# Splitting the squares of Q and K on GpSimd in place of VectorE, block by block

## The reference

```
dd = einsum('bhnd,md->bhnm', x * data_norm, proj)          # 8 heads of 64, 256 features
diag = 0.5 * sum(x * x, axis=-1) * data_norm ** 2          # per node and head
stab = max(dd) over the features (queries) or over nodes and features (keys)
out = ratio * (exp(dd - diag - stab) + 1e-4)
```

## Time and profile before

| What | Value |
|---|---|
| Median of 3 runs | 1333.23 us (1329.27 to 1333.36) |
| The profiled execution's own time | 1338.45 us |
| Its span | 1336.6 us |
| Mean granted TensorE clock | 0.957 of full speed |
| TensorE matmul busy | 1186.8 us, 89% |
| VectorE busy | 847.0 us, 63% |
| ScalarE busy | 311.2 us, 23% |
| GpSimd busy | 316.4 us, 24% |
| Q/K stage, layer 1 and layer 2 | about 83 to 146 us, about 523 to 587 us from the span's start |

### The profile page before, as it was taken

How to read it: one execution, slowest core, us unless ns; L and a number is a source line. 1 busy time by engine, 2 the same in 40 slices (tenths; PEclk the granted TensorE clock), 3 DMA queues, 4 the chain that set the end, 5 groups by cost and what they waited for, 6 DMA issues and landing times.

```text
span 1336.6 us, 16673 instructions
## 1 busy us (share of the span) xinstructions
PE 1186.8 (89%) x5940; PEld 936.6 (70%) x5960; DVE 847.0 (63%) x1727; ACT 311.2 (23%) x584; POOL 316.4 (24%) x223
## 2 busy tenths in 40 slices
PE   1699979999999989887999999997888899899695
PEld 0577879888788877677998878884434588687432
DVE  7767447769953366764777995335787415616766
ACT  2234334423111003443442311100111112011212
POOL 4420200104733313020010563240000143300306
PEclk9899789999999989998999999999999999899897
DMA  6400100101312110000010131142000010101001
GB/s 197 157 1 1 32 1 1 32 1 48 111 32 64 36 56 1 0 31 2 1 33 1 53 105 42 54 185 78 1 1 0 9 32 32 32 1 30 1 0 63
DMA packets 15786, 52.12 MB, mean 39 GB/s; under 512 B 2624, under 2 KB 3456, under 8 KB 15200
## 3 DMA queue, kind: packets, MB, share of 16 engines
q1 hardware_dynamic: 11488, 39.18, 9.0%
q10 hardware_dynamic: 4224, 11.91, 2.5%
HBM read 44.80 MB, written 6.29 MB: 38 GB/s over the span
## 4 chain that ended last, share of the span: by engine, by line
PE 55%; DVE 23%; issue 15%; ACT 4%; POOL 2%; DMA 1%; SPq 0%; POOLq 0%; DVEq 0%; ACTq 0%
PE ps_a L401 6%; PE ps_v L401 6%; PE ps_a L403 6%; PE ps_a L402 6%; PE ps_v L402 6%; PE ps_v L403 6%; PE ps_v L556 5%; PE ps_a L658 4%; DVE f_hi L1157 4%; PE ps_v L762 2%; PE ps_v L569 2%; DVE f_lo L1159 2%; DVE expk L1269 2%; DVE ht_lo L1159 2%; PE ps_a L422 2%
## 5 line engine op out<-in xcount | busy, mean ns | idle before, releaser
L401 PE MATMUL ps_a<-ht_hi,w_hi 128*128 128x512 f32 x496 | 195.1, 393 | 2.4 <-DVE most_i L1429 2.4
L402 PE MATMUL ps_a<-ht_lo,w_hi 128*128 128x512 f32 x496 | 193.7, 391 | 0.0
L403 PE MATMUL ps_a<-ht_hi,w_lo 128*128 128x512 f32 x496 | 193.6, 390 | 0.0
L978 POOL TENSOR_TENSOR w_lo<-stage,w_hi 128x1024 fp32r<-128x1024 f32 x58 | 148.8, 2566 | 32.8 <-issue 28.5
L786 ACT ACTIVATE work<-ps_a,col_sb 128x512 f32<-128x512 f32 x96 | 66.4, 719 | 331.4 <-PE ps_a L403 207.7
L976 POOL CAST w_hi<-stage 128x1024 fp32r<-128x1024 f32 x58 | 67.9, 1171 | 242.4 <-PE ps_a L403 138.5
L1343 DVE TENSOR_TENSOR xm<-ps_v,xm 128x512 f32<-128x512 f32 x80 | 55.2, 690 | 94.4 <-PE ps_v L403 94.0
L401 PE MATMUL ps_v<-w_hi,ht_hi 128*128 128x512 f32 x224 | 94.5, 422 | 21.6 <-issue 8.8
L401 PEld LDWEIGHTS ps_a<-ht_hi,w_hi 128*128 128x128 f32 x496 | 93.5, 189 | 24.4 <-issue 2.6
L403 PEld LDWEIGHTS ps_a<-ht_hi,w_lo 128*128 128x128 f32 x496 | 93.5, 189 | 19.9
L402 PEld LDWEIGHTS ps_a<-ht_lo,w_hi 128*128 128x128 f32 x496 | 93.6, 189 | 19.5
(11 more groups left out here) (190 smaller groups left out, 2208.0 us busy)
## 6 DMA issues: line engine op xcount, KB each, us to landing
stage<-wstream SPq DMA_DIRECT2D x62, 512.0 KB, 3.6
nat<-x ACTq DMA_DIRECT2D x8, 256.0 KB, 6.4
xt_d<-xt_hi SPq DMA_DIRECT2D x1, 2048.0 KB, 6.3
xt_d<-xt_lo SPq DMA_DIRECT2D x1, 2048.0 KB, 10.8
ht_hi<-xt_d ACTq DMA_DIRECT2D x1, 2048.0 KB, 9.6
ht_lo<-xt_d ACTq DMA_DIRECT2D x1, 2048.0 KB, 15.4
x_again<-x ACTq DMA_DIRECT2D x8, 256.0 KB, 4.2
out<-xm SPq DMA_DIRECT2D x8, 256.0 KB, 2.0
```

The costliest lines, as they stand in the source:

```text
L401: nc.tensor.matmul(ps, left[0], right[0], start=first, stop=False)
L402: nc.tensor.matmul(ps, left[0], right[1], start=False, stop=False)
L403: return nc.tensor.matmul(ps, left[1], right[0], start=False, stop=last)
L978: nc.gpsimd.tensor_tensor(lo, stage[:, j, :], hi.bitcast(f32), ALU.subtract).then_inc(w_split, 1)
```

## The change

The two instructions that split a block's squares move from VectorE's program to GpSimd's, for all 16 blocks of a layer. GpSimd takes the largest keys of pair 0 after the split of block 9, the weight `load(3)` after the split of block 15, and the largest keys of pairs 1 to 3 after that.

```
@@ GpSimd, mix_layer
-                for pair in range(NH // 2):
+                def largest_keys(pair):
                     pool.wait_ge(kmax_ready, L * (NH // 2) + (pair + 1))
                     hold(pool)
                     nc.gpsimd.partition_all_reduce(kall[:, pair, :], kmax1[:, pair, :], P, RMAX).then_inc(kall_ready, 1)
-                    if pair == 0:
-                        load(3, ("a", QK_ORDER[-1]))
+
+                def split_squares(n):
+                    pool.wait_ge(sq_ready, L * len(QK_ORDER) + (n + 1))
+                    hold(pool)
+                    nc.gpsimd.tensor_copy(sq_hi[:, n % 2, :], sq[:, n % 2, :]).then_inc(sq_high, 1)
+                    pool.wait_ge(sq_high, L * len(QK_ORDER) + (n + 1))
+                    nc.gpsimd.tensor_tensor(sq_lo[:, n % 2, :], sq[:, n % 2, :], sq_hi[:, n % 2, :].bitcast(f32),
+                                            ALU.subtract).then_inc(sq_split, 1)
+
+                for n in range(len(QK_ORDER)):
+                    split_squares(n)
+                    if n == 9:
+                        largest_keys(0)
+                load(3, ("a", QK_ORDER[-1]))
+                for pair in range(1, NH // 2):
+                    largest_keys(pair)
                 load(4, ("a", QK_ORDER[-1]))
@@ VectorE, mix_layer
-                def split_squares(n):
-                    dve.wait_ge(sq_ready, L * len(QK_ORDER) + (n + 1))
-                    nc.vector.tensor_copy(sq_hi[:, n % 2, :], sq[:, n % 2, :]).then_inc(sq_high, 1)
-                    dve.wait_ge(sq_high, L * len(QK_ORDER) + (n + 1))
-                    nc.vector.tensor_tensor(sq_lo[:, n % 2, :], sq[:, n % 2, :], sq_hi[:, n % 2, :].bitcast(f32),
-                                            ALU.subtract).then_inc(sq_split, 1)
-
@@ VectorE, mix_layer
                 for n in range(len(QK_ORDER)):
-                    split_squares(n)
                     low_parts(n)
```

## The result

| | Before | After |
|---|---|---|
| Median, both kernels measured side by side | 1333.3 us (1329.27 to 1341.8, 4 runs) | 1365.67 us (1363.81 to 1382.73, 4 runs) |
| Ratio, with its 95% interval | | 1.0263 (1.0167 to 1.0358) |
| The profiled execution, its span | 1338.45, 1336.6 us | 1363.81, 1361.9 us |
| Mean granted clock | 0.957 | 0.953 |

The change makes the kernel 2.6% slower; the forecast was 1360.6 us, 2.1% slower, in a range of 1350 to 1374.

What follows compares the result with a forecast made beforehand. TensorE, 89% busy, was taken to bound the kernel. Layer 1: 11.6 + 0.6 + 0.5 + 2.4 = 15.1; layer 2, less 2.8, 12.3; together +27.4 us on the median 1333.23: 1360.6 us, range 1350 to 1374.

Steps and rivals of the forecast that it cites:

- I take 0: VectorE's 32 roundings and 32 subtractions, 35.8 us: removing them gives no time back, as VectorE waits for ScalarE's high parts.
- The two loads: GpSimd loads other code around the reduction of pair 0's keys: 5.7 us into it, 6.9 out to elementwise work.
- Block 10's sum: TensorE's sum of block 10's squares waits for both loads: at 140.2 instead of 128.57, +11.6 us in each layer.
- Late splits: GpSimd's splits beside VectorE's low parts end 0.05 us late at each of ten exposed blocks: 0.5 us a layer.
- the other waits at L484: TensorE's waits for the squares, other than at blocks 10 and 15, were to stay under 0.2 us.
- Block 15: No product covers its split: 2.10 us on GpSimd against 1.5 on VectorE, +0.6 us a layer, TensorE waiting 2.4.
- Clock behind the stall: After block 10's stall TensorE runs at a lowered clock: 2.4 us lost in each layer, ends 0 and 6.5.
- Layer 2 regains 2.8: From block 10's sum to block 15's, layer 2 needs layer 1's 16.8 us instead of 19.6: -2.8 us.
- `load(3)` costs nothing: The weight starts behind block 15's split, about 160.5 instead of 143.27, done by 167.5, before pair 1's keys at 189: 0.
- Hidden loads: Rival: the idle stretches are a slow start after long idleness, leaving only 0.6 + 0.5 us a layer: 1335.4 us; chance 0.03.
- faster: Rival: loads cost nothing and layer 1's context products get full clock, -6.5 + 2.2 us: 1329 us; chance 0.03.
- Splits late and clock down: Rival: 0.4 us late at each exposed block, 8 us, perhaps layer 2's context products at 0.50: 1368 to 1374; chance 0.10.

Runs made afterwards that it cites:

- change_no_reduce: The change with GpSimd's four reductions over the partitions in each layer replaced by plain copies of kmax1 to kall: 1340.38 us, ratio to the kernel before 1.0008.
- change_again: The change itself once more, unaltered, with more rounds beside the kernel before: 1369.64 us, ratio to the kernel before 1.0254.
- before_no_reduce: The kernel before, with the same four reductions of each layer replaced by copies: 1345.02 us, ratio to the kernel before 1.0017.

## Why the prediction was right

It was right in the mechanism and in nearly every term.

- **"I take 0" for VectorE's 35.8 us.** Right. VectorE lost 34.8 us, and its low parts still wait for ScalarE's high parts in the change, 79.3 us in all. change_no_reduce shows the same: the splits are gone from VectorE, and the ratio to the kernel before is 1.0008.
- **The two loads, 5.7 and 6.9.** Measured 5.86 and 7.23 in layer 1, 5.83 and 6.95 in layer 2. The Trainium skill, GPSIMD Engine Reference, section Instruction dispatch, has about 6 us for a freshly loaded kernel: the way into the reduction agrees with it (5.5 to 6.3 in the runs here, but 6.5 to 6.8 where a needless reduction followed a weight's split at once), the way out to elementwise work is longer (6.6 to 7.7, and up to 8.2 in one place behind both layers).
- **Block 10's sum, +11.6 a layer, at 140.2.** It stood at 140.24, behind a wait of 11.76; layer 2 waited 11.45.
- **Late splits, 0.5 a layer.** The sum of the two layers, 1.0, came out at 1.06, but not as I put it. The steady blocks were not 0.05 late each: they kept their 3.22 us. Block 0 alone waited, 0.69 and 0.37. I had read block 4 and taken it for all. In the earlier trace rows there are 2.1 us from the end of block 4's square to its mask; at block 0 of the kernel before there are 1.55, from 84.12 to 85.67:

```profile
83.43 0.69 ACT L846 ACTIVATE sq<-ps_a,col_sb 128x512 f32<-128x512 f32 x1 [23.26 <-PE ps_a L403]
```

```profile
85.67 0.09 PEld L484 LDWEIGHTS ps_v<-sq_hi,headmask_r 128*8 128x8 f32 x1
```

  Here the reason failed and the size held by luck. It also breaks one sign of the forecast, that the other waits at L484 stay under 0.2.
- **Block 15, +0.6, a wait of 2.4.** It waited 2.53 in both layers, +0.69 and +0.70.
- **Clock behind the stall, 2.4 a layer.** 2.6 and 2.3.
- **Layer 2 regains 2.8.** It regained 3.2.
- **`load(3)` costs nothing.** It started at 159.86 (forecast 160.5) and ended at 166.7. The reduction of pair 1 was at 181.26, not 189: the context products ran at full clock. Pair 1's keys are waited for as before, for 4.82 us of TensorE's time at 184.04 beside 4.59 in the kernel before, and `load(3)` adds no wait.
- **The sum, +27.4.** The terms give 27.0. The profiled execution came to 1363.81 where I had 1365.9. That it came so near is in part luck: clock elsewhere gave 9.5 back and took 8.2, and neither stands in the sum; a gain at layer 1's context products was part of a rival only. Against the medians the change is 32.4 us slower in the first comparison and 27.7 in change_again; the first rests on four runs, and its interval holds both.
- **The rivals.** Hidden loads and faster: refuted by the wait itself. Splits late and clock down: the 0.4 us of the earlier trace rows did not meet these splits, whose subtraction took 1.251 to 1.299 us in all 32. The low parts beside them have one operand in PSUM. before_no_reduce has the counterpart, a VectorE subtraction with both operands in SBUF, where 0.69 became 2.71. No run moved an operand alone, so that the place of the operand decides it is not shown. The rival's other half, layer 2's first context products at half clock, stayed out in the change's profile (1.00 in both layers) and came in change_again's, with the same wait of 2.5 us ahead of them.

What stays open: what brings the clock down at the first context products and in the expert stage. It moves TensorE's time by 8 to 10 us in each place from one execution to the next, as much as many changes are worth, and with the wait ahead of one place filled the loss was gone there, came elsewhere in one profile, and the time did not measurably change.

## What to carry to other kernels

Before giving GpSimd a step that others wait for, look in its queue for what stands between the steps, not at its busy share: here 28% busy cost 2.6%, through two pauses of 6 to 7 us that already stood in the profile by "issue", where nothing waited for them. Such a pause belongs to the change from one kind of work to another, so group the kinds (no run here tried that alone), or make the change with a small needless call while GpSimd is idle, which gained 0.8% here. And work taken off an engine that itself waits gave nothing back here.

## What the runs showed of the hardware that I had not expected

- A needless reduction of a 128x4 tile takes the whole pause on itself: the real one behind it started 0.40 us later, when its input came.
- A rounding behind the reduction started at once (131.03), and only the subtraction behind that waited out the pause (7.23 us, until 138.94).
- GpSimd's subtraction of 128x1024 beside VectorE's of 128x512, all operands in SBUF, stretched VectorE's from 0.69 to 2.71 us and GpSimd's own hardly (2.40 in place of 2.35); GpSimd's rounding right behind it took 1.50 in place of 1.04.
- Fifty needless matmuls kept the granted clock at 1.00 through a stall behind which it had been 0.54.
